# A graph network with three edge convolutions on one core: two of them gather by slot instead of by tile

## The reference

```python
norm = dinv[src] * dinv[dst]
msg = h[src] * norm[:, None]            # h = x @ W
out = jax.ops.segment_sum(msg, dst, num_segments=n) + b
```

```python
e = leaky_relu(a_src[src] + a_dst[dst], NEG_SLOPE)
alpha = exp(e - e_max[dst]) / (segment_sum(e_exp, dst) + 1e-16)
out = segment_sum(h[src] * alpha, dst)
```

## Time and profile before

| | |
|---|---|
| median of 3 runs | 3417.91 us (3408.43 to 3418.81) |
| the profiled execution, its own time | 3414.29 us |
| its span, first to last instruction | 3412.6 us |
| mean granted PE clock | 0.772 of full speed |
| a1: first gather to last add | 502.64 to 1100.12 us |
| a2: first gather to last add | 1409.34 to 2002.13 us |
| a3: first gather to last gather | 2486.64 to about 3120 us |

### The profile page before, as it was taken

How to read it: one execution, slowest core, us unless ns; L and a number is a source line. 1 busy time by engine, 2 the same in 40 slices (tenths; PEclk the granted TensorE clock), 3 DMA queues, 4 the chain that set the end, 5 groups by cost and what they waited for, 6 DMA issues and landing times. The chain is left out here.

```text
span 3412.6 us, 35808 instructions
## 1 busy us (share of the span) xinstructions
PE 2259.6 (66%) x8719; PEld 1605.6 (47%) x8720; DVE 1748.6 (51%) x4031; ACT 388.2 (11%) x835; POOL 1376.5 (40%) x1300
## 2 busy tenths in 40 slices
PE   4108974455556788545555559999867777775597
PEld 3006753233324345323333337777655655564376
DVE  7457763344335774534343453333466666666443
ACT  1002220000001220100000022222211111110122
POOL 1820006767673120367676710000066666664100
PEclk9558986767667897777576669999977777777799
DMA  4201023333331000433333300000033333331000
GB/s 118 60 26 30 0 63 97 97 93 95 93 97 49 0 0 7 131 94 93 93 94 95 93 25 1 0 0 0 24 94 90 91 90 85 86 89 51 28 15 22
DMA packets 104762, 205.70 MB, mean 60 GB/s; under 512 B 33704, under 2 KB 63323, under 8 KB 104572
## 3 DMA queue, kind: packets, MB, share of 16 engines
q0 software_dynamic: 60304, 169.70, 18.4%
q1 hardware_dynamic: 44396, 35.29, 3.5%
HBM read 187.91 MB, written 16.73 MB: 60 GB/s over the span
## 5 line engine op out<-in xcount | busy, mean ns | idle before, releaser
L393 POOL DMA_INDIRECT BIG<-table,CSTB x784 | 794.5, 1013 | 796.4 <-DMA table<-ACC 458.5
L535 PE MATMUL PB<-BIG,OH 128*128 x1664 | 630.1, 531 | 558.7 <-issue 355.1
L535 PEld LDWEIGHTS PB<-BIG,OH 128*128 128x128 f32 x1664 | 396.5, 261 | 792.3 <-issue 732.4
L381 POOL DMA_INDIRECT BIG<-table,SRCI x416 | 428.6, 1030 | 715.4 <-DMA table<-ACC 512.4
L1204 DVE TENSOR_TENSOR ACC<-ACC,PB 128x256 f32 x832 | 350.1, 421 | 652.9 <-issue 241.5
L745 PE MATMUL PB<-BIG,WA 128*128 128x264 f32 x832 | 295.6, 504 | 126.7 <-DVE BIG L1477 54.7
L745 PEld LDWEIGHTS PB<-BIG,WA 128*128 128x128 f32 x832 | 187.3, 243 | 192.3 <-issue 81.6
L1507 DVE TENSOR_TENSOR ACC<-ACC,PB 128x264 f32 x416 | 176.9, 425 | 152.3 <-remote 83.9
L1406 DVE SCALAR_TENSOR_TENSOR X<-PB,SMALL,X 128x256 f32 (+1 forms) x200 | 96.7, 484 | 220.8 <-PE PB L678 220.8
L1477 DVE TENSOR_TENSOR BIG<-BIG 128x256 f32<-128x256 f32 x416 | 156.7, 418 | 76.5 <-ACT BIG L911 53.9
L669 PE MATMUL PB<-XT,WA 128*128 128x320 f32 x640 | 187.2, 449 | 7.5 <-DVE X L1413 7.5
(11 more groups left out here) (337 smaller groups left out, 2370.7 us busy)
## 6 DMA issues: line engine op xcount, KB each, us to landing
table<-ACC SPq DMA_DIRECT2D x20, 660.0 KB, 3.4
BIG<-table,CSTB POOLq DMA_INDIRECT x784
BIG<-table,SRCI POOLq DMA_INDIRECT x416
X<-in_x SPq DMA_DIRECT2D x1, 3072.0 KB
out<-X SPq DMA_DIRECT2D x4, 640.0 KB
WA<-in_L_ffn_w SPq DMA_DIRECT2D x1, 2048.0 KB
WB<-in_L_ffn_w SPq DMA_DIRECT2D x1, 2048.0 KB
BIG<-wtab SPq DMA_DIRECT2D x1, 1600.0 KB, 6.2
```

The source lines that it names most:

```text
L381: g.indirect_dma_start(out=G[:, k * ROW:(k + 1) * ROW], out_offset=None, in_=table, in_offset=bass.IndirectOffsetOnAxis(ap=SRCI[:, n:n + 1 ...
L393: g.indirect_dma_start(out=GT[:, k * ROW:(k + 1) * ROW], out_offset=None, in_=table, in_offset=bass.IndirectOffsetOnAxis(ap=TSRC[:, n:n + ...
L535: pe.matmul(PB[k][:, 0:width], OH[:, ((q % 2) * GRP + k) * P:((q % 2) * GRP + k + 1) * P], GT[:, ds(t, width)], start=True, stop=True).the ...
```

## The change

- `a1` and `a2` gather by slot with `gather_slots`: 416 gathers instead of 392, 32 places in the ring instead of 48, indices from `SRCI`. An edge tile that has two slots is gathered twice.
- PE's matmuls read constant places. The load of 8 registers for each group, the copies of registers and `TROW` are gone. PE waits for the group of gathers that it reads (`a1_in0` to `a1_in3`), for all 52 groups.
- POOL's wait before gather n of a group is for n - 24 slots done instead of n - 16. This holds for a1, a2 and a3.
- The loops of PE and DVE in a1 and a2 have 13 turns of 4 groups.
- Out of the setup go two loads of `tile_src` on SP, a memset, six small operations, a cast (L1088) and the copies L1092 and L1093 on DVE, and eight small PE operations (L476, L479).
- SP's wait for the end of a2 ahead of the attention vectors' load is gone.
- The gather at the start that nobody uses is gone.

```diff
-            g.memset(IDX[:, :], 0).then_inc(sem("idx_zero"), 1)
-            g.wait_ge(sem("idx_zero"), 1)
-            g.indirect_dma_start(out=BIG[:, 0:D], out_offset=None, in_=a["x"],
-                                 in_offset=bass.IndirectOffsetOnAxis(ap=IDX[:, :], axis=0)).then_inc(sem("first_gather"), 16)
-            g.wait_ge(sem("first_gather"), 16)
...
-            def gather_slots(tb, st):
+            def gather_slots(tb, st, ring, width, rows):
+                if st == "a1":
+                    g.wait_ge(sem("slots_ready"), 1)
                 g.wait_ge(sem("table_stored"), (GNNS.index(tb) + 1) * NC * 16)
                 for n in range(SLOTS):
                     q = n // GRP % NG
                     if n % GRP == 0:
-                        g.wait_ge(sem(f"{st}_mm"), BODY + n - 2 * GRP)
+                        g.wait_ge(sem(f"{st}_mm"), n + GRP)
                     k = n % BODY
-                    g.indirect_dma_start(out=G[:, k * ROW:(k + 1) * ROW], out_offset=None, in_=table,
+                    g.indirect_dma_start(out=ring[:, k * width:(k + 1) * width], out_offset=None, in_=rows,
                                          in_offset=bass.IndirectOffsetOnAxis(ap=SRCI[:, n:n + 1], axis=0)).then_inc(sem(f"{st}_in{q}"), 16)
-            gather_tiles("g1", "a1")
+            gather_slots("g1", "a1", G, ROW, table)
...
-            gather_tiles("g2", "a2")
-            gather_slots("g3", "a3")
+            gather_slots("g2", "a2", G, ROW, table)
+            gather_slots("g3", "a3", G, ROW, table)
...
-                pe.matmul(PB[3][0:1, k * P:(k + 1) * P], SLF[:, 8 + k:9 + k], IDENT[:, :], start=True, stop=True)
-            pe.wait_ge(sem("tile_rows"), 1)
-            for k in range(4):
-                mm = pe.transpose(PB[7][:, k * P:(k + 1) * P], tile_srcf[:, k * P:(k + 1) * P], IDENT[:, :])
...
-                def body(i, groups, tiles):
-                    for q in range(groups):
-                        n0 = (i * TG + q) * GRP
-                        if q < tiles:
-                            pe.wait_ge(sem(f"tiles_in{q}"), 16 * GRP * (i + 1 + (st == "a2") * groups_at(q)))
-                        pe.wait_ge(sem(f"{st}_oh"), i * TG + q + 1)
-                        pe.load(regs, TROW[0:1, ds(n0, GRP)])
+                with pe.Fori(0, TURNS) as i:
+                    for q in range(NG):
+                        pe.wait_ge(sem(f"{st}_in{q}"), 16 * GRP * (i + 1))
+                        pe.wait_ge(sem(f"{st}_oh"), i * NG + q + 1)
                         for k in range(GRP):
-                            t = pe.snap(regs[k], min_val=0, max_val=(RING - 1) * ROW)
-                            pe.wait_ge(sem(f"{st}_acc"), BODY + n0 + k + 1 - GRP)
+                            pe.wait_ge(sem(f"{st}_acc"), BODY + i * BODY + q * GRP + k + 1 - GRP)
                             pe.matmul(PB[k][:, 0:width], OH[:, ((q % 2) * GRP + k) * P:((q % 2) * GRP + k + 1) * P],
-                                      GT[:, ds(t, width)], start=True, stop=True).then_inc(sem(f"{st}_mm"), 1)
-                with pe.Fori(0, S_GROUPS // TG) as i:
-                    body(i, TG, TG)
-                body(S_GROUPS // TG, S_GROUPS % TG, T_GROUPS % TG)
+                                      G[:, (q * GRP + k) * ROW:(q * GRP + k) * ROW + width], start=True, stop=True).then_inc(sem(f"{st}_mm"), 1)
```

More of the change, by code:

```diff
@@ L29 @@
 BODY = GRP * NG
-TG = 6
-RING = TG * GRP
 TURNS = SLOTS // BODY
-T_GROUPS = ET // GRP
-S_GROUPS = SLOTS // GRP
 LN_EPS = 1e-5
@@ L46, in tiles_before @@
     return NT * ORDER.index(st)
-def groups_at(q):
-    return (T_GROUPS - q + TG - 1) // TG
 def rows_before(st):
@@ L108, in build @@
         DREL = sb("DREL", [P, SLOTS + GRP * NG])
-        IDX = sb("IDX", [P, 1], I32)
         WROW = sb("WROW", [1, 512], I32)
-        TROW = sb("TROW", [1, 512], I32)
         IDENT = sb("IDENT", [P, P])
@@ L144, in build @@
         G = BIG[:, 0:BODY * ROW]
[L145 to L148, removed]
         RANKROW = BIG[:, 5120:5120 + NT * P]
@@ L227, in _ @@
             sp.dma_start(dst2, a["dst"].rearrange("(p c) -> p c", p=P)).then_inc(sem("ld_dst"), 16)
-            sp.wait_ge(sem("x_padded"), 2)
+            sp.wait_ge(sem("x_padded"), 1)
             sp.dma_start(X[:, 0:(NT - 1) * D].rearrange("p (t c) -> p t c", c=D),
@@ L234, in _ @@
                 sp.dma_start(IDN[:, NT:2 * NT], a["src"][0:NT * P].rearrange("(t p) -> p t", p=P)).then_inc(sem("ld_idn"), 16)
-            sp.dma_start(tile_src[:, 0:3 * P].rearrange("p (k e) -> p k e", k=3), a["src"][0:3 * P * P].rearrange("(k p e) -> p k e", k=3, p=P)).then_inc(sem("ld_tsrc"), 16)
-            sp.dma_start(tile_src[0:ET - 3 * P, 3 * P:4 * P], a["src"][3 * P * P:ET * P].rearrange("(p e) -> p e", e=P)).then_inc(sem("ld_tsrc"), 16)
             wg = WG[:, :].rearrange("p (b c) -> p b c", b=KB)
@@ L306, in _ @@
             sp.dma_start(wg[:, :, 0:D], a["L3_gnn_W"].rearrange("(b p) h d -> p b (h d)", p=P)).then_inc(sem("ld_wg"), 16)
-            sp.wait_ge(sem("a2_mm"), BODY + SLOTS)
             sp.dma_start(CSTB[:, 0:D], a["L3_gnn_att_src"].rearrange("h d -> (h d)").partition_broadcast(P)).then_inc(sem("ld_wg"), 16)
@@ L521, in sum_slots @@
                 pe.sem_inc(sem(f"{st}_mm"), BODY)
-                regs = [pe.alloc_register(f"{st}_tile{k}") for k in range(GRP)]
-                def body(i, groups, tiles):
-                    for q in range(groups):
-                        n0 = (i * TG + q) * GRP
-                        if q < tiles:
-                            pe.wait_ge(sem(f"tiles_in{q}"), 16 * GRP * (i + 1 + (st == "a2") * groups_at(q)))
-                        pe.wait_ge(sem(f"{st}_oh"), i * TG + q + 1)
-                        pe.load(regs, TROW[0:1, ds(n0, GRP)])
+                with pe.Fori(0, TURNS) as i:
+                    for q in range(NG):
+                        pe.wait_ge(sem(f"{st}_in{q}"), 16 * GRP * (i + 1))
+                        pe.wait_ge(sem(f"{st}_oh"), i * NG + q + 1)
                         for k in range(GRP):
-                            t = pe.snap(regs[k], min_val=0, max_val=(RING - 1) * ROW)
-                            pe.wait_ge(sem(f"{st}_acc"), BODY + n0 + k + 1 - GRP)
+                            pe.wait_ge(sem(f"{st}_acc"), BODY + i * BODY + q * GRP + k + 1 - GRP)
                             pe.matmul(PB[k][:, 0:width], OH[:, ((q % 2) * GRP + k) * P:((q % 2) * GRP + k + 1) * P],
-                                      GT[:, ds(t, width)], start=True, stop=True).then_inc(sem(f"{st}_mm"), 1)
-                with pe.Fori(0, S_GROUPS // TG) as i:
-                    body(i, TG, TG)
-                body(S_GROUPS // TG, S_GROUPS % TG, T_GROUPS % TG)
-                for r in regs:
-                    pe.free_register(r)
+                                      G[:, (q * GRP + k) * ROW:(q * GRP + k) * ROW + width], start=True, stop=True).then_inc(sem(f"{st}_mm"), 1)
             pe.wait_ge(sem("ld_wg"), 16)
@@ L944, in _ @@
             v.memset(X[:, (NT - 1) * D:NT * D], 0.0).then_inc(sem("x_padded"), 1)
-            v.memset(tile_src, 0).then_inc(sem("x_padded"), 1)
             line.mark(v.memset(ZEROB[:, :], 0.0))
@@ L1071, in _ @@
             v.tensor_copy(SLI[:, :], SLF[:, 8:12]).then_inc(sem("slot_tile"), 1)
[L1073 to L1078, removed]
             line.mark(v.tensor_scalar(SLF[:, 4:8], SLF[:, 0:4], float(ROW), None, ALU.mult))
@@ L1086, in _ @@
             ins.then_inc(sem("slot_rows"), 1)
-            v.wait_ge(sem("ld_tsrc"), 32)
-            v.tensor_copy(tile_srcf, tile_src).then_inc(sem("tile_rows"), 1)
             v.wait_ge(sem("slotsT"), 1)
@@ L1091, in _ @@
             v.tensor_copy(DREL[:, 0:SLOTS], PB[5][:, 0:SLOTS])
-            v.tensor_copy(TSRC[:, 0:ET + GRP], PB[7][:, 0:ET + GRP])
-            v.tensor_copy(TROW[:, :], PB[3][0:1, 0:512])
             v.memset(SRCI[:, SLOTS:], 0)
@@ L1194, in body @@
                     for q in range(groups):
-                        n0 = (i * TG + q) * GRP
+                        n0 = i * BODY + q * GRP
                         v.wait_ge(sem(f"{st}_mm"), BODY + n0)
@@ L1204, in body @@
                             v.tensor_tensor(dst, dst, PB[k][:, 0:width], ALU.add).then_inc(sem(f"{st}_acc"), 1)
-                with v.Fori(0, S_GROUPS // TG) as i:
-                    body(i, TG)
-                body(S_GROUPS // TG, S_GROUPS % TG)
+                with v.Fori(0, TURNS) as i:
+                    body(i, NG)
                 v.wait_ge(sem(f"{st}_acc"), BODY + SLOTS)
```

## The result

The changed kernel takes 3471.84 us (median of 4 runs, 3467.99 to 3486.06), the kernel before 3417.99. Over all executions the ratio is 1.0172, 95% interval 1.0138 to 1.0205. Forecast was 3390.5, with a range from 3325 to 3458.

A forecast was written before the change was run, and what follows sets the result against it. POOL's issuing of gathers was taken to set the pace. Gathers, stalls and tails brought a1 + a2 from 1190.3 to 1169.8 us (-20.5); with the setup -23.8, from 3414.3 to 3390.5 us, range 3325 to 3458.

The forecast's parts named there:

- 24 more gathers at 1.300 us: In a1 and a2 each: 416 gathers instead of 392, without stalls 540.8 and 541.1 us instead of 509.6 and 509.9.
- The lead halves the stalls: POOL's waits for slots in a1 and a2: with lead 24, stalls come half as often, 59.9 us instead of 119.8.
- Rival B: Stalls in a1 and a2 stay in proportion, 119.8 us, the lead brings nothing; whole 3450.4 us, slower; chance 0.22.
- The tail: Work behind the last gather of a1 and a2: 14 us each, 28 instead of 57.9 in all.
- the upper bound: Tail of a1 or a2: 24 slots left at the end, 17.4 us, some 5 more in a slow part.
- a3 at 0: a3, where only the lead changes: holes 10 us longer but half as often, so 0, bounds 0 and +30.
- The setup: Chain ending in `slots_ready`: fewer matmul pairs, transposes and copies on PE and DVE save 3.3 us.
- The unused gather at 0: At the start: dropping it is worth 0, at most a few tenths; the first used gather takes 46.70 us regardless.
- C: Stalls in a1 and a2 vanish because PE's register loads and addresses start the sluggish phases; whole 3330.6 us; chance 0.20.
- D: Borders of loop turns in a1 and a2 cost 4.3 us each, 112 us at stake; whole 3446 to 3502; chance 0.10.

The follow-up runs named there:

- e18: Kernel before (392 gathers, lead 16), but PE waits only for the tile group it needs, on chip 1: 3169.6 us, 0.9885 of before.
- e1: Changed kernel with POOL's wait back to n - 16 slots in a1, a2 and a3, chip 12: 3446.4 us, 1.0072 of before.
- e2: Changed kernel with the wait for n - 16 slots in a3 alone, chip 12: 3474.8 us, 1.0163 of before.
- e12: Changed kernel with the wait for n - 16 slots in a1, a2 and a3, chip 3: 3468.9 us, 1.0025 of before.
- e15: The kernel before, unchanged, run for its own profile on chip 12: 3413.4 us.
- e16: Kernel before (392 gathers, lead 16), but PE waits only for the tile group it needs, chip 12: 3423.7 us, 0.9997 of before.
- e3: Changed kernel with DVE's adds in a1 and a2 at constant places, no row registers, chip 12: 3452.7 us, 1.0084 of before.
- e4: Changed kernel with PE's and DVE's loops in a1 and a2 written out, chip 12: 3471.1 us, 1.0133 of before.
- e9: The changed kernel as it is, on chip 5: 3504.1 us, 1.0102 of before.
- e10: Changed kernel with gathers of a1 and a2 fetching a quarter of the bytes, chip 5: median unusable (two executions 434 us apart), only its profile is used.
- e11: The changed kernel as it is, on chip 3: 3499.9 us, 1.0114 of before.
- e13: Changed kernel with the wait for n - 16 slots in a1 and a2, n - 24 in a3, chip 3: 3487.2 us, 1.0072 of before.
- e14: Kernel before with the wait for n - 24 slots in a3 alone, chip 3: 3467.7 us, 1.0006 of before.
- e5: Kernel before with the wait for n - 24 slots in a3 alone, chip 6 (without stalls): 3207.0 us, 1.0001 of before.
- e8: Changed kernel with a1's and a2's loops written out and adds at constant places, chip 6 (without stalls): 3214.0 us, 1.0019 of before.
- e17: Kernel before with the wait for n - 8 slots in a1, a2 and a3, chip 12: 3611.0 us, 1.0535 of before.

## Why the prediction was wrong

The profiled execution came 81.7 us over the forecast: 53.2 by the stalls, 9.5 by the tails, 17.8 by a3, 1.5 by the setup, and small ones.

**24 more gathers at 1.300 us.** Right: forecast 540.8 and 541.1 without stalls, measured 540.9 and 542.1. The chip without stalls gives 32.3 and 25.9 us for them.

**The lead halves the stalls: wrong, and this is the step that failed.** Forecast 59.9 us over both convolutions, measured 57.5 + 55.6 = 113.1, so 53 us of the miss. I took from one period a rate for catching up and one for falling back, had the period grow from 34.4 to some 74 us with the lead, and held the length of a stall fixed. The period didn't grow: in a1 and a2 there are 15 waits over 1 us in the mean with a lead of 16 and 15 with 24, and none of the profiles with 24 has as few as half. Rival B, the stalls stay in proportion (119.8), was near; it had 0.22. Its sum of 3450.4 took the tails and a3 over from my forecast; both moved the same way, and so the measured time lies 14 us above the range that ended a little over it.

**The tail.** Mis-sized: 14 each forecast, 16.5 and 21.0 measured, 9.5 us in all. On the chip without stalls it is 10.1 (with the lead of 16). The rest may be backlog, as the upper bound had it; no run separates it. My reason for the long tail of before was only half right: I named the 24 slots beyond the last tile and the lead. e18 shows that what held the slots back, on a chip without stalls, was waits for tiles that they don't read, since with exact waits the tail is 11 us with 392 gathers.

**a3 at 0.** Measured +17.8, inside the bound of +30. Over fourteen profiles on chips with stalls, a3 was 642 to 660 us with a lead of 16 (before, e1, e2, e12, e15, e16) and 649 to 696 with 24 (after, e3, e4, e9, e10, e11, e13, e14), 653 against 681 in the mean, though the chips are mixed in unevenly. a3 of the kernel before has three holes over 6 us (9.8, 8.6 and 8.6), as I had read, but they aren't all: DVE's idle stretches over 4 us there are 12, where a3 on the chips without stalls has one, at its start; POOL waits 58.4 + 28.9 = 87.3 us for slots, and a3 is 104 us longer than in e5. I had let the holes get longer by some 10 us and come half as often. The longest idle stretch of DVE in a3's gathers is 8.2 to 11.1 us in the six profiles with 16 and 12.2 to 16.5 in the eight with 24, and those over 4 us are 12 to 15 with 16 and 14 to 23 with 24: longer, but not rarer. The longest of the changed kernel (start, length, idle before it in brackets):

```profile
2570.78 0.76 DVE L1415 TENSOR_TENSOR BIG<-BIG 128x256 f32<-128x256 f32 x2 [13.58 <-ACT BIG L861]
```

This agrees with holes that last until POOL stops; that e2 and e14 show nothing of it in their medians doesn't. So the lead costs something, 31 us in e11 against e12, and how much of that is a3's stays open.

**The setup.** Mis-sized: 3.3 forecast. From the start of the first gather that is used to the first operation of the attention weights it takes 207.96 - 76.64 = 131.3 us before and 207.12 - 77.64 = 129.5 after, so 1.8 us. Of the missing 1.5, 0.7 can be the next point. The first operation of the attention weights, before and after:

```profile
207.96 0.26 DVE L1104 TENSOR_TENSOR SMALL<-ACC,BIG 128x100 f32<-128x100 f32 x1
```

```profile
207.12 0.26 DVE L1043 TENSOR_TENSOR SMALL<-ACC,BIG 128x100 f32<-128x100 f32 x1
```

**The unused gather at 0.** It was worth 0.7 us. The first used gather took 46.70 us with it and 47.38 without it:

```profile
77.64 47.38 POOL L337 DMA_INDIRECT BIG<-table,IDN  x1 [75.45 <-DMA table<-ACC]
```

It is 46.70 or 46.71 in all seven profiles with the unused gather and 47.38 to 47.40 in all thirteen without it, on both kinds of chip.

**The rivals.** C fell with the changed kernel itself: PE's queue is clean and the stalls are there. e15 shows the same for the kernel before. D fell with e4 and e8: without any loop turns a1 took 613.1 us on one kind of chip and 546.8 on the other, within 2 us of the kernels with turns (614.9 and 548.7); e8 has the constant rows as well.

## What to carry to other kernels

Ask of a stall that returns with a period what stays fixed when the buffer in front of it grows: its length, its number or its sum. One period shows none of the three; I took the length from it. From 8 slots of lead to 16 the sum stayed and the stalls got longer, from 16 to 24 in a1 and a2 number and sum stayed about as they were, and the longer lead bought nothing. Where the queue that sets the pace pays for each item, 6% more items cost more than simpler waits give back (15 and 8 us here); look for the exact wait first, which here gave the short tail without the items (0.9885 where the chip doesn't stall). And profile a kernel on more than one chip before explaining its stalls.

## What the hardware showed that I had not expected

The same program took 3208.8 and 3206.2 us on chips 6 and 1, 3424.5 and 3423.1 on chip 12 at two times, 3465.1 on chip 3 and 3467.9 on chip 5. On the latter three, instructions of DVE's queue that take 21 to 51 ns on the former take up to 1396 ns in a1 and a2 (1411 in e11), most of the slow ones near 700, in phases that end about when POOL's gathers pause. The stalls that go with the phases don't depend on the gathers' bytes (96 or 24 GB/s), on registers or on loops.

The slow instructions can't be the whole of it. In a3 the same copy of a row register is never slow, in the same execution of the kernel before, and POOL waits 87.3 us for slots there; with a lead of 8 it is slow in a1 at most a few times:

```profile
L1503 DVEq FUSED_REGOPS  x384: 51/51/58, 2504.5 to 3097.6; - x192
```

What these stalls have in common is that DVE takes up PE's results late. (Not so in a3 of e17: there one add of 416 is late, and the short lead itself makes the waits.) In a1 of e17, PE has ended 8 slots at 641.30, by the profile's modelled ends. DVE adds the third of them at 640.53 and the fourth only at 645.43, though the profile shows nothing that it still needs, 2.1 us behind the end of POOL's last gather:

```profile
635.96 5.34 PE L535 MATMUL PB<-BIG,OH 128*128 x16 [4.77 <-issue]
640.53 0.42 DVE L1204 TENSOR_TENSOR ACC<-ACC,PB 128x256 f32 x1 [1.95 <-PE PB L535]
642.34 0.95 POOL L393 DMA_INDIRECT BIG<-table,CSTB  x1 [0.30 <-issue]
645.43 0.42 DVE L1204 TENSOR_TENSOR ACC<-ACC,PB 128x256 f32 x1 [4.48 <-remote]
646.44 0.94 POOL L393 DMA_INDIRECT BIG<-table,CSTB  x1 [3.16 <-remote]
```

Counted over a1: adds that start more than 1.5 us after their matmul and DVE's operation before have both ended are 76 of 416 in the kernel before, 86 in the changed one, 90 in e3 and 30 in e17. On the chips without stalls there is none, in any convolution of any profile. What holds the results back, and what differs between the chips, no run shows.
